# A cross-interaction ranking tower on one core: paired TensorE products in four column quarters instead of two halves, and gathers that wait for TensorE's progress

## What is computed

```python
e = stack([tbl_f[ids[:, f]] for f in range(32)], axis=1)      # (1024, 32, 32): batch, field, dim
x = e
for W in (W0, W1):                                            # (32*32, 128), (32*128, 128)
    z = einsum('bhd,bmd->bhmd', e, x).reshape(b, -1, 32)
    x = einsum('bpd,pj->bjd', z, W)
    res.append(x)
z = sum(concatenate(res, axis=1), axis=-1)                    # (1024, 256)
h = concatenate([z, dense_ctx], axis=1)                       # (1024, 272)
h = maximum(h @ W_top1 + b_top1, 0); h = maximum(h @ W_top2 + b_top2, 0)
y = h @ W_top3                                                # (1024, 1)
```

## Time and profile before

| what | value |
|---|---|
| median of three executions | 380.32 us (378.18 to 383.03) |
| profiled execution: span from first to last instruction | 597.7 us |
| profiled execution: its own time around the span | not given by the profile |
| mean granted TensorE clock over the span | 0.80 of full speed |
| TensorE matmul busy in the span | 412.6 us |
| gathers on GpSimd | 256, 960 ns each |

### The profile page before, as it was taken

One profiled execution on the slowest core, in us unless ns is written; L12 is line 12 of the kernel. 1 busy time (PEld: TensorE's weight loads), 2 busy tenths in 40 slices (PEclk: granted clock), 3 DMA queues, 4 the chain that ended last, 5 costly groups with the idle time before them and its releaser, 6 DMA issues.

```text
span 597.7 us, 9512 instructions
## 1 busy us (share of the span) xinstructions
PE 412.6 (69%) x3656; PEld 360.8 (60%) x3656; DVE 203.4 (34%) x834; ACT 235.5 (39%) x774; POOL 246.5 (41%) x262
## 2 busy tenths in 40 slices
PE   5512112874257887877788778687787679999988
PEld 4301001653256776766666667577676668989988
DVE  4200000694723333322333233333332235556510
ACT  3300000662175334522343334433452237676641
POOL 6777772547055444544445554544444440000000
PEclk9755555795589877877787888977787779999999
DMA  8100000000000000000000000000000000000000
GB/s 299 45 14 13 13 13 6 11 3 14 2 10 10 8 10 7 10 8 9 9 9 10 10 10 9 11 8 9 8 10 8 8 10 2 2 2 2 2 2 1
DMA packets 10765, 9.66 MB, mean 16 GB/s; under 512 B 4664, under 2 KB 8896, under 8 KB 10720
## 3 DMA queue, kind: packets, MB, share of 16 engines
q0 software_dynamic: 8192, 4.21, 4.8%
q1 hardware_dynamic: 2528, 4.84, 2.3%
HBM read 9.03 MB, written 0.00 MB: 15 GB/s over the span
## 4 chain that ended last, share of the span: by engine, by line
PE 57%; issue 18%; another core or an unknown queue 11%; DVE 7%; ACT 6%; DMA 1%; SPq 0%; ACTq 0%
PE WA L725 20%; PE QB L697 10%; PE PA L687 8%; PE T L710 4%; DVE RT L421 4%; PE M L738 4%; PE M L757 2%; PE ET L674 2%; ACT eblk L285 2%; ACT TS L285 1%; PE PA L639 1%; PE M L764 1%; PE M L748 1%; ACT RT L285 1%
## 5 line engine op out<-in xcount | busy, mean ns | idle before, releaser
L278 POOL DMA_INDIRECT emb<-in_table,rows x256 | 245.8, 960 | 239.0 <-PE ET L674 165.3
L725 PE MATMUL WA<-TS,RX 128*128 128x128 f32 x896 | 127.0, 301 | 1.0 <-ACT TS L285 1.0
L584 DVE COPY TS<-T 32x64 f32<-32x64 f32 x256 | 55.5, 217 | 200.6 <-PE T L710 184.6
L725 PEld LDWEIGHTS WA<-TS,RX 128*128 128x128 f32 x896 | 119.7, 215 | 6.0 <-issue 6.0
L697 PE MATMUL QB<-eblk,zQ 128*64 128x68 f32 x1024 | 69.1, 243 | 74.3 <-issue 74.0
L697 PEld LDWEIGHTS QB<-eblk,zQ 128*64 128x64 f32 x1024 | 49.9, 146 | 89.8 <-issue 85.8
L552 DVE TENSOR_TENSOR zQ<-ET,eT 128x1024 f32<-128x1024 f32 x32 | 39.2, 1225 | 159.0 <-ACT eT L285 158.9
L687 PE MATMUL PA<-eblk,zP 128*128 128x132 f32 x512 | 80.6, 296 | 5.3 <-issue 3.4
L639 PE MATMUL PA<-sym,TS 128*128 128x272 f32 x64 | 29.4, 552 | 74.5 <-issue 47.3
L687 PEld LDWEIGHTS PA<-eblk,zP 128*128 128x128 f32 x512 | 73.4, 212 | 6.3 <-issue 4.9
L285 ACT ACTIVATE eblk<-ET 32x256 f32<-32x256 f32 x128 | 48.6, 380 | 71.0 <-PE ET L674 66.0
(11 more groups left out here) (87 smaller groups left out, 294.1 us busy)
## 6 DMA issues: line engine op xcount, KB each, us to landing
emb<-in_table,rows POOLq DMA_INDIRECT x256
TS<-in_W SPq DMA_DIRECT2D x8, 256.0 KB, 4.3
wt<-in_W_top SPq DMA_DIRECT2D x2, 512.0 KB
y1w<-in_W_rows SPq DMA_DIRECT2D x1, 448.0 KB
TS<-in_W_rows SPq DMA_DIRECT2D x1, 448.0 KB
sym<-in_W_cols SPq DMA_DIRECT2D x1, 264.0 KB, 2.8
TS<-in_W_cols SPq DMA_DIRECT2D x1, 264.0 KB, 3.1
idc<-in_ids SPq DMA_DIRECT2D x1, 128.0 KB, 2.0
```

What stands on the lines that cost most here:

```text
L278: eng.indirect_dma_start(emb[par][:, g, :], None, table, bass.IndirectOffsetOnAxis(rows[:, k, g:g + 1], 0))\
L584: eng.tensor_copy(view(ts[32 * q:32 * q + 32, :, :], P * REST + b0, [[4 * P, 2], [P, 4], [1, 8]]), view(src, q, [[C17, 2], [4, 4], [C33, 8 ...
L725: m = eng.matmul(WA[:, 0:P], C[:, kt, :], TS[k % 2][:, slot_of(kt), :], start=(kt == 0), stop=(kt == KT - 1))
```

## The change

Two edits. The matmuls of `across_triples` are cut in four quarters of 32 columns instead of two halves of 64: the same weights and the same places of QB; the 68 columns of a half are now streamed once for each of its two quarters. And each gather from the seventeenth on waits for a count of TensorE's progress. With n the number of the gather from 0: n = 0 to 15 go as before; n = 16 to 27 wait until 2(n-16)+9 channels of the weight product are made; n = 28 on wait for `p_made` of (n-28)·3 // 8 + 1 trios. The wait for `et_made` stays.

```diff
         EARLY_AT = (8, 18)
+        FREE, PACED = 16, 12
...
                     for g in range(UG * unit, UG * unit + UG):
+                        n = GROUPS * UNITS * k + g
+                        if FREE <= n < FREE + PACED:
+                            eng.wait_ge(rt_made, 2 * (n - FREE) + F - 2 * PACED + 1)
+                        elif n >= FREE + PACED:
+                            eng.wait_ge(p_made, (n - FREE - PACED) * TRIOS // UG + 1)
                         eng.indirect_dma_start(emb[par][:, g, :], None, table,
...
                     at = NQ * C17 * (g % 4)
-                    for X in range(2):
-                        m = eng.matmul(QB[g // 4][64 * X:64 * X + 64, at:at + NQ * C17].rearrange("p (v c) -> p v c", c=C17),
-                                       zQ[u % 2][:, g, X, :], eblk[u % 2][:, g, :, C17 * (1 - X):C17 * (2 - X)],
+                    for j in range(NQ):
+                        X, y0 = j // 2, 32 * (j % 2)
+                        m = eng.matmul(QB[g // 4][32 * j:32 * j + 32, at:at + NQ * C17].rearrange("p (v c) -> p v c", c=C17),
+                                       zQ[u % 2][:, g, X, y0:y0 + 32], eblk[u % 2][:, g, :, C17 * (1 - X):C17 * (2 - X)],
                                        start=True, stop=True)
```

## The result

The changed kernel takes 382.06 us (median of 20 runs, 380.15 to 386.36), the kernel before 378.43 (20 runs, 376.94 to 383.23): a ratio of 1.0097, 95% interval 1.0074 to 1.012. It is 1% slower, where the forecast was 2.3 us of gain on the 380.3 us then known, 378 us. The value lies inside the range of 367 to 388, on the other side of no change.

The account below looks back on a forecast made before the run. TensorE's path, built at 365 us, was taken as the bound, with GpSimd's gathers equal within error. Quarters -1.3, gates +2 and stall -3 summed to -2.3 on 380.3: 378 us, range 367 to 388.

Parts of the forecast that it names:

- the gates: Gathers waiting for TensorE's progress, mainly by trios in tile 0: cost between 0 and 11 us, taken as +2.
- the stall: TensorE idle up to 9 us beside gathers, mainly in early weight products; pacing gains 0 to 10 us, taken as -3.
- the quarters: Four column quarters in across_triples: same block length, 0.96 us between first and last start; gain 1.3 us, bounds 0 and 3.
- The 15 us: Timed median 380.3 less built span 365: time around the span plus any real stall; limit of what pacing can win.
- my built path: Kernel's span built from undisturbed rows, without the stall: tile 1 at 89, seven tiles of 36.3, last 21.8; 365 us.
- The twelve gates by weight products: Gathers 16 to 27, waiting for channels: 0 to 2 us of delay, hidden by a lead of several units.
- Rival 3: Gathers held at tile 0's sums lose nine gathers of lead, never won back: +11 less 1.3, 390 us; chance 0.10.
- The 4.13 us gather: One gather slowed beside VectorE's long sums, held for 3.2 us; taken as evidence against lost lead.
- Rival 1: Stall beside gathers is real in timed runs; pacing takes 10 us, the hand-over gives 1.3: 369 us; chance 0.21.
- rival 4: Gates do nothing because GpSimd is always behind, quarters give 0 to 3: 377 to 380; chance 0.62 jointly with forecast.
- rival 2: Quarters bound by issue at 25 ns a matmul: 1.64 us a block instead of 0.96, +22 us, 399; chance 0.07.
- The hand-over: Step from L697's block to L710's, 0.17 us: 0.1 won in one unit of four, 0.02 in three; 1.3 us total.

Follow-up runs that it names:

- second profile: The kernel before, unchanged, profiled once more: one execution, 376.74 us, span 374.9 us, last gather starting at 331.5 us.

## Why the prediction was right or wrong

**The step that failed: the gates and the stall in the sum, +2 and -3.** Each was priced by a reading that the runs contradict. By the ratios of the runs the gates cost 3.9 us instead of 2, the stall gives 0 instead of 3, and the quarters 0 instead of 1.3: slower by 3.7 us, where 2.3 us of gain were forecast. That 378 is close to the median of before in 20 runs, 378.43, is luck: the three runs from which it was reckoned lay 2 us too high.

- The stall: I left it up to 10 us of the median and took 3 as a gain. Nothing of it is left in the second profile. The 15 us that I could not place were not stall. The span's own margin is 1.8 us, the true medians are 2 us lower than the three runs shown, and nearly all the rest is GpSimd: without it at the end the span is 366.1, where my built path says 365. The path was right (tile 1 begins at 89.8 in that run, at 89 in mine); it wasn't what bounds the kernel.
- The gates: the case that applied was the one I set aside, that GpSimd is the slower one in the steady tiles, and a microsecond lost anywhere is lost at the end. I had noted that gathers end at 324 and are needed at 325, "equal within my error", and then priced the gates as if the lead were there. The argument that a late GpSimd finds the gates open was half right: behind 95.45 us they cost next to nothing (all 27 waits at the trio gates come to 5.1 us beyond the steps' own, and two of them make 4.6 of it). But they close in tile 0 and among the weight products, before it is late. Measured: +2.8 us in the last gather for the gates by weight products, +4.6 for those by trios, and 1.0104 as a ratio for both.
- The twelve gates by weight products, "0 to 2 us of delay, hidden by a lead of several units": the size was about right (2.6 us of waits), the word hidden was wrong.

**Rival 3 (lost lead)** had the right mechanism and the sign, and I gave it 0.10. Its size was too large: 11 us for the gates by trios, against 5.1 us at them in the changed kernel's profile, 4.6 in the last gather of the gates by trios alone, and some 4 in the medians of the whole change. Of the nine gathers to be lost at tile 0's wait, only the gates at 89.73 and 95.45 took much, 1.33 and 3.23 us above a step's idle time: the sums had already stretched gathers, so that in the second profile of before GpSimd has begun 62 gathers at 90 us and not 69. The 4.13 us gather, which I held against it, thus cuts both ways: such sums make the gates cost less than 11 us, and they are why GpSimd has no lead to give away at the end.

**Rival 1 (the stall is real)** is out by the second profile of before, **rival 4 (the gates do nothing)** by the gates alone. The forecast had joined rival 4 with itself; the two should have been split by sign. (Its price for rival 2 has a slip: 380.3 + 22 - 1.3 is 401, not 399.)

**Quarters.** The block's length was right to 0.01 us (1.17 against 1.18). The hand-over was read rightly and counted a little too high. Where nothing else holds the block behind, in the fourth unit of a tile, the step went from 0.15 to 0.04 us, the 0.1 that I had given it. In the other three I had given it 0.02 each, and ScalarE's copies leave nothing: the block behind starts 0.19 us after the last narrow matmul (108.26 + 1.17 - 0.22 = 109.21 to 109.40), no sooner than after the last wide one. So it is 0.1 us a tile, 0.8 in all instead of 1.3, and it reaches the time only where TensorE sets the end; where GpSimd does, nothing. The drain that the Trainium skill's page TensorEngine Tiling (Array Packing), Key Properties, gives to a change of tiling mode agrees with the 0.15 and 0.04 us; the 3 us that I gave by it would have needed all 32 units. **Rival 2 (quarters bound by issue)** is out: 64 matmuls start in 1.17 - 0.22 = 0.95 us, 15 ns apart. The Trainium skill's page TensorE: Matmul & The Clock Gate gives about 25 ns as the least distance, which would have made that 1.6 us; the measurement decides against it for matmuls that run in different columns of the array.

**What was to be shown by the profile.** The span fell by far more than 50 us and the median hardly moved, as I wrote; but that said nothing of the change, since the unchanged kernel's span falls as far. The sign for rival 3, transposes that wait for gathers in later tiles, is there: ten units, 10.4 us. But the kernel before has it too, with five units and 4.8 us; the difference, 5.6 us, is what speaks for the gates.

## What to carry to other kernels

When the profiled execution is far from the timed ones, profile the same kernel again before reading a mechanism from it. When two engines come out equal at the end, price a wait on either at its full length there, and split the chances by sign: a lead counts as cover only if it is still there at the last unit. And a producer that runs without a pause, and whose last piece the end waits for, is a bound, however idle the page makes it look: 67% busy here, with a fixed 0.30 us between instructions.

## What was not expected of the hardware

- An indirect gather of 128 rows is as regular as a clock: 0.94 to 0.95 us and 0.30 us of idle, from the third to the last, except beside VectorE operations with both inputs in SBUF, where it took from 1.0 to 4.1 us and once 5.83.
- 64 matmuls of 32 weight columns in four column quarters start 15 ns apart, and the step to the next block of 32 columns took 0.04 us, where it took 0.15 from a block of 64.
- One execution took 597.7 us of span, with TensorE idle for up to 9 us at a time while gathers went on. No other profile or timed run did it. What caused it stays open.
